# A three-phase decoder layer: self-attention body wrapped to sixteen steps, cross-attention steps reordered, combining stage split over three engines

## Chip, cores and metric

The kernel runs on one core of a Trainium2 chip. The metric is the device time of one execution in microseconds, lower is better. A core has a matrix engine (PE), and three engines for the rest: DVE (VectorE), ACT (ScalarE) and POOL (GpSimd). SP is the queue that issues transfers. Engines run their own instruction lists in order and wait for each other through semaphores.

## What is computed

Sixteen sequences of 256 tokens with 256 features pass through one decoder layer. Cut to its steps:

```python
def layer(x, ctx, mask):
    xn   = layer_norm(x) * w + b
    q, k, v, p, y = split(xn @ W_in.T + b_in)       # 16 heads of 32, k smeared with the token before
    pos  = cumsum(sigmoid(y))                       # forget gates, an additive bias of the scores
    a    = causal_softmax(q @ k.T * scale + pos) @ v * silu(p)
    x1   = layer_norm(x + layer_norm(a @ W_out.T))
    kv   = cat(layer_norm(ctx), layer_norm(x1))     # 512 keys, those of ctx under the mask
    o    = softmax(q2(x1) @ k2(kv).T / 8) @ v2(kv)  # 16 heads of 64
    x2   = layer_norm(x1 + o @ Wo)
    out  = layer_norm(x2 + moe(x2))                 # 8 experts, the best two of each token
```

## The kernel before

Three functions follow each other: `self_phase`, `cross_phase`, `expert_phase`. Each phase but the last loops over the 16 sequences, one pass for each. Products that need more than one float32r pass are split products: an operand is kept as a high and a low part, and three products replace one (L783 in the self-attention, L1566 in the cross-attention). Transposes, value products and the output projection are whole float32 products.

**Self-attention.** A pass has a step for each of 16 units (a unit is one head) and a few more steps in which nothing but the last units' tail is left. PE in a step: a piece of a projection of the next sequence (L783), transposes of probabilities (`transposes`, L831), the scores of the next unit (L823), and after each fourth unit a value product (L842, L849). ACT takes exponentials (L431) and transposed probabilities (L437), and takes the projections out of PSUM. DVE masks scores (L673, L675), gates, takes values and normalises. The next sequence's input is transposed (L791) near the start of a pass; its first user is the product L774, which reads `xn_t`.

**Cross-attention.** A pass has 32 units (one of 16 heads, one half of the queries) in 16 pairs, and 19 steps on PE; I write, with the lines of before, for pair i:

- S(i): the scores of pair i, six split products (`scores`, L1633). It fills both score banks, so it waits until the masked scores of pair i-1 are done.
- M(i): two masked copies on DVE, from the banks into two slots of `prob` (`masked_scores`, L1409), with the reciprocal of pair i-1's sums between them and two multiplications behind them (`probabilities`, L1420). ACT follows with the exponentials (L1219).
- T(i): eight transposes of pair i's probabilities (`transposes`, L1645), which ACT copies out (L1225). V(m): a value product after every second pair (`values`, L1662).
- P: a piece of a split projection of the next sequence (L1566), `kq`, `first` and `second` in the code.

PE runs T(i-2) and S(i+1) in step i. The `prob` slots form a ring of six, three pairs. So a masked copy also waits for transposes:

```python
apart(pt_filled, pt_filled.at(b, u - PROB_RING + 1))
apart(score_filled, score_filled.at(b, u + 1))
```

For pair i that is T(i-3), which PE runs in the same step as S(i). DVE carries other work between the pairs: the sum and statistics of the layer norm in step 3, `best_two` (the routing choice) in step 8, `list_places` in step 10. ACT takes the transposed context and latents in steps 4 and 5 (L1247, L1251).

**Experts.** After the expert rounds, a combining stage goes over 16 blocks: DVE adds the two expert rows and x2 (L2178, L2183), takes statistics (L2188, L2192) and normalises (L2200); POOL computes the reciprocal root.

Of the kernel before, what the change touches and what calls it, by code (L numbers as in the profile page):

```python
# [12 lines left out]
ALU = mybir.AluOpType  # L13
# [58 lines left out]
def decoder_layer(nc, x, ctx_in, mask, w_in_t, w_out_t, wq, wkv, wout, cols, rows, heads_rows, y_bias, wr,  # L72
                  w1, b1, w2, b2, out):
    x1_dram = nc.dram_tensor("x1_rows", (T + S, D), F32).ap()
# [3 lines left out]
    with stack:  # L78
# [14 lines left out]
        with ExitStack() as inner:  # L93
# [16 lines left out]
            cross_phase(nc, sem, passed, sig, ctx_in, mask, x1_dram, x2_dram, list_dram, ident, vx, pt, wq_s, wkv_s, wox, wr_s, col,  # L110
# [4 lines left out]
def self_phase(nc, sem, passed, sig, x, w_in_t, w_out_t, wq, wkv, wout, wr, cols, rows, heads_rows, y_bias, x1_dram, list_dram,  # L115
# [4 lines left out]
    XT, YP, QP, WO, KP, PP, VP = 0, 1, 2, 4, 6, 8, 10  # L120
    LNS = LN_X, LN_OUT, LN_RES = range(3)
    PROB_RING, PT_RING = 6, 2 * EC
    with ExitStack() as stack:
# [53 lines left out]
        v_a = sb("v_a", [P, TC, D_EXP])  # L177
        p_tanh = sb("p_tanh", [P, EC, S])
# [11 lines left out]
        x_res = sb("x_res", [P, TC, D])  # L190
        out_s = sb("out_s", [P, TC, D])
        centred = sb("centred", [P, TC, D])
# [16 lines left out]
        x_loaded, again_loaded = sig("x_loaded", 16), sig("again_loaded", 16, 0)  # L209
        parts_loaded = [sig(f"parts_loaded{g}", 16 * 8) for g in range(HPC)]  # L210
        x1_stored = sig("x1_stored", 16)
# [12 lines left out]
        zx_ready, x_res_ready, x1_ready = sig("zx_ready", 1), sig("x_res_ready", 1), sig("x1_ready", 1)  # L224
# [12 lines left out]
        gate_scaled = sig("gate_scaled", HPC)  # L237
        pt_filled = sig("pt_filled", HEADS)
# [9 lines left out]
        def gate_columns_of(w, k):  # L248

            return w[:, k, 3 * D_EXP:4 * D_EXP].rearrange("p (m g d) -> p g m d", g=HPC, m=EC)  # L250

# [4 lines left out]
        def _(sp):  # L256
# [14 lines left out]
            def spread_q_and_pos(b, g):  # L271
                sp.wait_ge(score_filled.sem, score_filled.at(b, EC * g + EC))
                spread_to(q_parts, g, (q_hi, q_lo, q_hi))
# [4 lines left out]
            def spread_early(b):  # L278

                sp.wait_ge(q_split.sem, q_split.at(b, 2))  # L280
                sp.wait_ge(pos_steps.sem, pos_steps.at(b, 4))
                for g in range(HPC - 1):
                    spread_q_and_pos(b, g)
                sp.wait_ge(k_split.sem, k_split.at(b, 2))
                for g in range(HPC - 1):
                    spread_to(k_parts, g, (k_hi, k_hi, k_lo))

            def spread_last(b):
                g = HPC - 1
                spread_q_and_pos(b, g)  # L290
                spread_to(k_parts, g, (k_hi, k_hi, k_lo))
# [13 lines left out]
            spread_early(-1)  # L305
            spread_last(-1)
# [5 lines left out]
            with sp.Fori(0, B) as b:  # L312
                pass_wait(zx_ready, zx_ready.at(b, 1))
                sp.dma_start(x_raw[:], rows_of((b + 2) % B)).then_inc(x_loaded.sem, 16)
                pass_wait(x_res_ready, x_res_ready.at(b, 1))
                sp.dma_start(x_again[:], rows_of(b)).then_inc(again_loaded.sem, 16)
                spread_early(b)
                pass_wait(x1_ready, x1_ready.at(b, 1))
                sp.dma_start(x1_dram.rearrange("(b c p) d -> b p c d", c=TC, p=P)[b], x1[:]).then_inc(x1_stored.sem, 16)
                spread_last(b)  # L320
            sp.wait_ge(x1_ready.sem, x1_ready.at(B, 1))
            sp.dma_start(x1_dram.rearrange("(b c p) d -> b p c d", c=TC, p=P)[B], x1[:]).then_inc(x1_stored.sem, 16)
# [3 lines left out]
            sp.wait_ge(x_loaded.sem, x_loaded.at(B, 16))  # L326
            for g in range(HPC):
                sp.wait_ge(parts_loaded[g].sem, parts_loaded[g].at(B - 1, parts_loaded[g].per))
# [3 lines left out]
        def _(pool):  # L332
# [41 lines left out]
            def residual(b):  # L374

                pool.wait_ge(again_loaded.sem, again_loaded.at(b, 16))
                pool.wait_ge(residual_ready.sem, residual_ready.at(b - 1, 1))
                pool.tensor_tensor(x_res[:], x_again[:], onb.unsqueeze(1).broadcast_to([P, TC, D]), ALU.add).then_inc(x_res_ready.sem, 1)

            pool.sem_inc(x_res_ready.sem, 1)  # L380
            for s in (var_ready, rstd_ready):
                for ln in (LN_OUT, LN_RES):
                    pool.sem_inc(s[ln].sem, 1)
            reciprocal_root(-1, LN_X)
            pool.wait_ge(in_weights, N_IN)
            low_q(-1)
            low_k(-1)
            reciprocal_root(0, LN_X)
            with pool.Fori(0, B) as b:
                residual(b)  # L390
                low_q(b)
                for ln in (LN_OUT, LN_RES):
                    reciprocal_root(b, ln)
                low_k(b)
                reciprocal_root(b + 1, LN_X)
            residual(B)
            for ln in (LN_OUT, LN_RES):
                reciprocal_root(B, ln)
# [3 lines left out]
        def _(act):  # L402
# [49 lines left out]
            def take_q(b, n):  # L452
                f = QP + n
                if n == 0:
                    act.wait_ge(q_split.sem, q_split.at(b - 1, 2))
                    for g in range(HPC):
                        act.wait_ge(parts_loaded[g].sem, parts_loaded[g].at(b - 1, parts_loaded[g].per))
                filled(b, f)
                for dst in (q_t, q_hi):
                    for i in range(2):  # L460
                        m = 2 * n + i
                        ins = nc.scalar.activation(dst[:, m, :], proj[f % 2][:, i * S:(i + 1) * S], ACT.Identity,
                                                   bias=q_bias[:, m:m + 1], scale=q_scale[:, m:m + 1])
                taken(ins, f)
# [10 lines left out]
            def high_k(b, n):  # L475
                f = KP + n
                act.wait_ge(proj_taken[f % 2].sem, proj_taken[f % 2].at(b, f // 2 + 1))
# [19 lines left out]
            def projections(b):  # L497
                take_xt(b)
                take_y(b)
                for n in range(2):  # L500
                    take_q(b, n)
                for n in range(2):
                    smear_k(b, n)
                    high_k(b, n)
                for n in range(2):
                    tanh_p(b, n)

            for s in (exp_ready, *pt_taken):
                act.sem_inc(s.sem, s.per)
            projections(-1)  # L510
            steps = {1: [take_xt], 2: [take_y], 3: [lambda b: take_q(b, 0)], 4: [lambda b: take_q(b, 1)],
                     5: [take_output(0)], 6: [take_output(1)], 7: [lambda b: smear_k(b, 0)], 9: [lambda b: smear_k(b, 1), lambda b: high_k(b, 0)],
                     11: [lambda b: high_k(b, 1)], 12: [lambda b: tanh_p(b, 0)],
                     14: [lambda b: tanh_p(b, 1)]}
            with act.Fori(0, B) as b:
                for i in range(HEADS + 3):
                    if i < HEADS:
                        exps(b, i)
# [1803 lines left out]
```

## Time and profile before

| | us |
|---|---|
| median of 3 runs (2789.85 to 2791.23) | 2791.01 |
| the profiled execution | 2794.18 |
| its span, first to last instruction | 2792.4 |
| PE busy, share of the span | 2442.5 (87%) |
| DVE busy | 1903.6 (68%) |
| ACT busy | 1736.8 (62%) |
| POOL busy | 806.5 (29%) |

The mean granted clock of TensorE was 0.956 of full speed. Time zero of the rows is the first instruction; an idle time in brackets stands ahead of the instruction and names what ended it. A matmul's own length overlaps with the next one, so the distance between two starts is what a piece of work costs PE.

### The profile page before, as it was taken

The page shows a single profiled execution, that of the slowest core. Times are in us where ns is not written, and L with a number is a line of the kernel's source. Part 1 is how long each engine was busy: PE and PEld are TensorE (multiplying, and loading weights), DVE is VectorE, ACT ScalarE, POOL GpSimd, SP SyncE. Part 2 cuts the span into 40 slices and gives each one's busy share as a digit, 9 for nine tenths or more (in the row PEclk, how much of TensorE's full clock was granted, in tenths as well). Part 3 has the DMA queues.
Part 4 walks back from the last instruction along what each step waited for, and adds up shares of the span by engine and source line. Part 5 has one row for each costly group of instructions (what it writes and reads, how often), then busy time and mean ns, then how long its engine had stood idle before and what let it go on. Part 6 is the DMA issues. An engine that isn't in the chain of part 4 may idle for free. (4 is left out here: it accounts for less than half of the span.)

```text
span 2792.4 us, 62033 instructions
## 1 busy us (share of the span) xinstructions
PE 2442.5 (87%) x18114; PEld 2021.8 (72%) x18114; DVE 1903.6 (68%) x5382; ACT 1736.8 (62%) x4354; POOL 806.5 (29%) x852
## 2 busy tenths in 40 slices
PE   5878887887599999999999999999999469999990
PEld 3666666666477777777777777777777369999990
DVE  4676667666556677666776667766677268888857
ACT  3777777777445666666666666666566156767650
POOL 1221212211333332333222332223332224444422
PEclk8999999999799999999999999999999789999995
DMA  5644544544300000000000000000000167777746
GB/s 143 151 98 106 113 94 113 113 95 111 80 16 9 9 15 16 16 15 2 16 16 16 16 4 14 15 16 16 9 9 15 43 197 237 233 233 236 234 148 229
DMA packets 162415, 228.14 MB, mean 82 GB/s; under 512 B 34544, under 2 KB 129136, under 8 KB 161776
## 3 DMA queue, kind: packets, MB, share of 16 engines
q1 hardware_dynamic: 151248, 205.85, 26.6%
q0 software_dynamic: 9664, 20.53, 2.1%
q14 instruction: 105, 0.86, 0.1%
q10 hardware_dynamic: 1376, 0.54, 0.1%
q8 instruction: 22, 0.36, 0.1%
HBM read 140.71 MB, written 23.74 MB: 59 GB/s over the span
## 5 line engine op out<-in xcount | busy, mean ns | idle before, releaser
L1409 DVE CUSTOM_DVE_ANT_0 x_prob<-x_score,x_mask_add 128x512 f32<-128x512 f32 x512 | 348.0, 682 | 275.4 <-PE x_score L1633 216.5
L1219 ACT ACTIVATE x_prob<-x_prob,x_low 128x512 f32<-128x512 f32 x512 | 366.9, 720 | 208.5 <-DVE x_low L1409 205.9
L1225 ACT COPY x_pt<-x_ptb 128x512 f32<-128x512 f32 x512 | 273.0, 584 | 240.9 <-PE x_ptb L1645 237.9
L1146 POOL TENSOR_TENSOR x_k_lo<-x_whole,x_k_hi 128x512 fp32r<-128x512 f32 x136 | 174.9, 1286 | 440.5 <-ACT x_k_hi L1265 438.1
L431 ACT ACTIVATE prob<-prob,low 128x128 f32<-128x128 f32 (+1 forms) x512 | 229.9, 455 | 103.8 <-DVE low L675 103.8
L1420 DVE TENSOR_SCALAR x_prob<-x_prob,x_rden 128x512 f32<-128x512 f32 x512 | 281.3, 591 | 0.6
L1645 PE MATMUL x_ptb<-ident,x_prob 128*128 128x128 f32 x2048 | 266.2, 273 | 0.0
L1662 PE MATMUL x_av<-x_pt,x_vx 128*64 128x256 f32 x2048 | 249.3, 385 | 0.0
L1645 PEld LDWEIGHTS x_ptb<-ident,x_prob 128*128 128x128 f32 x2048 | 230.3, 141 | 7.9 <-issue 5.8
L1389 DVE COPY x_whole<-x_proj 128x512 f32<-128x512 f32 x204 | 138.6, 686 | 128.5 <-PE x_proj L1566 127.0
L1662 PEld LDWEIGHTS x_av<-x_pt,x_vx 128*64 128x64 f32 x2048 | 135.7, 136 | 99.2 <-issue 43.8
L2026 ACT ACTIVATE h_t<-h_bank,b_s 128x256 f32<-128x256 f32 x312 | 130.8, 470 | 114.5 <-PE h_bank L2245 106.1
L2245 PE MATMUL h_bank<-xg_hi,w_hi 128*128 128x256 f32 x624 | 177.5, 284 | 21.5 <-DVE xg_lo L2106 20.1
L2245 PE MATMUL h_bank<-xg_hi,w_lo 128*128 128x256 f32 x624 | 177.3, 284 | 0.0
L2245 PE MATMUL h_bank<-xg_lo,w_hi 128*128 128x256 f32 x624 | 177.2, 284 | 0.0
L2259 PE MATMUL y_bank<-w_hi,h_hi 128*128 128x256 f32 x624 | 176.7, 283 | 0.0
L2259 PE MATMUL y_bank<-w_lo,h_hi 128*128 128x256 f32 x624 | 175.2, 281 | 0.0
L2259 PE MATMUL y_bank<-w_hi,h_lo 128*128 128x256 f32 x624 | 174.7, 280 | 0.0
L1566 PE MATMUL x_proj<-x_keys_hi,x_wkv_hi 128*128 128x256 f32 x544 | 164.4, 302 | 7.8 <-POOL x_keys_lo L1132 5.7
L1981 POOL DMA_INDIRECT expert_rows<-y_s,tokens x78 | 100.5, 1289 | 244.7 <-DVE y_s L2141 226.6
L673 DVE CUSTOM_DVE_ANT_0 prob<-score,causal 128x128 f32<-128x128 f32 x256 | 73.7, 288 | 124.8 <-PE score L823 119.3
L437 ACT COPY pt<-ptb 128x384 f32<-128x384 f32 x256 | 118.9, 471 | 64.0 <-PE ptb L831 64.0
(264 smaller groups left out, 7320.5 us busy)
## 6 DMA issues: line engine op xcount, KB each, us to landing
w_s<-w SPq DMA_DIRECT2D x156, 512.0 KB, 4.7
q_parts<-q_hi SPq DMA_DIRECT2D x136, 128.0 KB, 2.4
k_parts<-k_hi SPq DMA_DIRECT2D x136, 128.0 KB, 2.3
q_parts<-q_lo SPq DMA_DIRECT2D x68, 128.0 KB, 2.4
k_parts<-pos_parts SPq DMA_DIRECT2D x136, 64.0 KB, 2.4
k_parts<-k_lo SPq DMA_DIRECT2D x68, 128.0 KB, 2.4
w_s<-expert_rows SPq DMA_DIRECT2D x16, 512.0 KB, 4.3
b_s<-b SPq DMA_DIRECT2D x39, 128.0 KB
```

Source lines behind the costliest of these rows:

```text
L431: ins = nc.scalar.activation(s, s, ACT.Exp, bias=low[:, u, c:c + 1], scale=-1.0, accum_out=den[:, u, c:c + 1])
L1146: pool.tensor_tensor(part_of(n, q_lo, k_lo), whole_of(n), part_of(n, q_hi, k_hi).bitcast(F32), ALU.subtract).then_inc(low_ready.sem, 1)
L1219: nc.scalar.activation(slot, slot, ACT.Exp, bias=low[:, u:u + 1], scale=-1.0, accum_out=den[:, u:u + 1]).then_inc(exp_ready.sem, 1)
L1225: nc.scalar.copy(pt[:, u % PX_RING, :], ptb[u % 2][:, :]).then_inc(pt_taken[u % 2].sem, 1)
L1389: taken(dve.tensor_copy(whole[:, n % WHOLES, :], proj[f % 2][:, :]), f)
L1409: dve.tensor_tensor_reduce(prob[:, u % PROB_RING, :], score[u % 2][:, :], mask_add[:, :], -X_SCALE, 3.0e38, ALU.add, ALU.min, low[:, u:u + ...
L1420: ins = dve.tensor_scalar(slot, slot, rden[:, u:u + 1], None, ALU.mult)
L1566: ins = matmul(out, lhs(i, k), rhs(j, k), start=(k == 0 and i + j == 0), stop=(k == KC - 1 and i == 1))
L1645: ins = transpose(ptb[o][:, n * P:(n + 1) * P], prob[:, u % PROB_RING, n * P:(n + 1) * P], ident[:])
L1662: ins = matmul(av[m % 2][DH_X * o:DH_X * (o + 1), 0:S], vx[:, n, DH_X * h:DH_X * (h + 1)], pt[:, u:u + 3:2, n * P:(n + 1) * P], start=(n = ...
L2245: ins = matmul(h_bank[m][:, n * SLOTS:(n + 1) * SLOTS], w[a][:, k, f * P:(f + 1) * P], xs[z][:, k, :], start=(k == 0 and a + z == 0), stop ...
L2259: ins = matmul(y_bank[i][:, c * D:(c + 1) * D], h[a][:, f, c * P:(c + 1) * P], w[z][:, f, :], start=(f == 0 and a + z == 0), stop=(f == FC ...
```

## The change

**Self-attention.** The loop body has exactly 16 steps. With a lag of three, the transposes, the values and the takes of units 13 to 15 stand in the first steps of the next pass. The output chain (projection, statistics, residual, x1, store) of a sequence moves one pass later, spread over the pass. Values go to `v_next` first and POOL copies them to `v_a`. The normalisations of x and x1, the low part of xn and the residual's bias move from DVE to POOL. The `prob` ring shrinks from 6 to 4. The last pass is written out by itself, without a next sequence's projections.

**Cross-attention.** In each PE step the scores of the next pair and the split products come first, then the transposes, values and the other whole products. The tables of DVE, ACT and POOL stay. The last pass is written out by itself, without a next sequence's projections and normalisations.

**Combining stage.** The x2 blocks are loaded early, into expert weight buffers that are no longer used. The normalisation moves from DVE to ACT, and POOL computes a shift beside the reciprocal root.

```diff
--- before
+++ after
@@ self_phase @@
-    XT, YP, QP, WO, KP, PP, VP = 0, 1, 2, 4, 6, 8, 10
+    XT, YP, KP, QP, WO, PP, VP = 0, 1, 2, 4, 6, 8, 10
-    PROB_RING, PT_RING = 6, 2 * EC
+    PROB_RING, PT_RING = 4, 2 * EC
+    LAG = 3
@@ self_phase, POOL @@
+            def low_x(b):
+                pool.wait_ge(xn_hi_ready.sem, xn_hi_ready.at(b, 1))
+                pool.tensor_tensor(xn_lo[:], xn_t[:], xn_hi[:].bitcast(F32), ALU.subtract).then_inc(xn_split.sem, 1)
+            def values_in_place(b):
+                pool.wait_ge(av_done.sem, av_done.at(b - 1, HPC))
+                for f in (VP, VP + 1):
...
+                    pool.tensor_copy(v_a[:, f - VP, :], v_next[:, f - VP, :]).then_inc(v_ready.sem, 1)
+            def x1_of(b):
+                reciprocal_root(b, LN_RES)
+                pool.wait_ge(x1_stored.sem, x1_stored.at(b, 0))
+                normalise(LN_RES, x1, res1, x1_ready, b)
@@ cross_phase, PE @@
-            before_ = {1: second[1], 2: second[2], 4: last_values_and_context, 5: latents_transposed, 6: x2_transposed,
-                       8: kq[1], 9: kq[2], 10: kq[3], 11: kq[4], 12: kq[6], 13: kq[7], 14: kq[8], 15: kq[9], 16: kq[10],
-                       17: kq[11], 18: first[3]}
-            after_ = {0: second[0], 1: output, 6: kq[0], 7: logits, 9: prefixes, 11: kq[5], 13: first[0], 15: first[1],
-                      17: first[2]}
+            split_parts = {0: [second[0]], 1: [second[1]], 2: [second[2]], 4: [second[3]], 7: [kq[0]], 8: [kq[1]], 9: [kq[2]],
+                           10: [kq[3]], 11: [kq[4], kq[5]], 12: [kq[6]], 13: [kq[7], first[0]], 14: [kq[8]], 15: [kq[9], first[1]],
+                           16: [kq[10]], 17: [kq[11], first[2]], 18: [first[3]]}
+            whole_parts = {1: [output], 4: [context_transposed, latents_transposed], 5: [x2_transposed], 7: [logits], 9: [prefixes]}
             scores(0, 0)
-            with pe.Fori(0, B) as b:
+            def one_pass(b, split, whole, more):
                 for i in range(HEADS + 3):
-                    if i in before_:
-                        before_[i](b)
+                    if i + 1 < HEADS:
+                        scores(b, i + 1)
+                    elif i == HEADS + 2 and more:
+                        scores(b + 1, 0)
+                    for part in split.get(i, ()):
+                        part(b)
                     if 2 <= i < HEADS + 2:
                         transposes(b, i - 2)
-                    if i + 1 < HEADS:
-                        scores(b, i + 1)
-                    elif i == HEADS + 1:
-                        scores(b + 1, 0)
                     if i >= 4 and i % 2 == 0:
                         values(b, (i - 4) // 2)
-                    if i in after_:
-                        after_[i](b)
+                    for part in whole.get(i, ()):
+                        part(b)
...
+            with pe.Fori(0, B - 1) as b:
+                one_pass(b, split_parts, whole_parts, True)
+            one_pass(B - 1, {0: [second[0]], 1: [second[1]], 2: [second[2]], 4: [second[3]]},
...
@@ expert_phase, SP @@
+            for b in range(BLOCKS):
+                load_x2(b)
+            for n, tiles in enumerate((N_TILES - RING, N_TILES - RING, N_TILES - RING + 1)):
+                sp.wait_ge(h_filled.sem, h_filled.at(tiles, FC // 2))
+                for b in range(BLOCKS * (n + 1), BLOCKS * (n + 2)):
+                    load_x2(b)
```

The first place is PE's list in the cross-attention, step 10 of a pass (`x_score` rows are S(11), `x_ptb` rows T(8), `x_av` rows V(3), `x_proj` rows P). Before, the last product of the step's P stands first:

```order
L1566 MATMUL x_proj<-x_keys_hi,x_wkv_lo 128x256
L1643 REGISTER_ALU
L1645 MATMUL x_ptb<-ident,x_prob 128x128 x8
L1625 REGISTER_ALU
L1633 MATMUL x_score<-x_k_hi,x_q_hi 128x512 x2
L1633 MATMUL x_score<-x_k_hi,x_q_lo 128x512 x2
L1633 MATMUL x_score<-x_k_lo,x_q_hi 128x512 x2
L1662 MATMUL x_av<-x_pt,x_vx 64x256 x8
```

And now, from the end of the step's P to the scores of the next step, S(12); S(11) stands ahead of that P:

```order
L1680 MATMUL x_proj<-x_keys_hi,x_wkv_lo 128x256
L1757 REGISTER_ALU
L1759 MATMUL x_ptb<-ident,x_prob 128x128 x8
L1776 MATMUL x_av<-x_pt,x_vx 64x256 x8
L1739 REGISTER_ALU
L1742 REGISTER_ALU
L1747 MATMUL x_score<-x_k_hi,x_q_hi 128x512 x2
L1747 MATMUL x_score<-x_k_hi,x_q_lo 128x512 x2
L1747 MATMUL x_score<-x_k_lo,x_q_hi 128x512 x2
```

The scores have moved from behind the transposes to the head of the step, so between T(8) and the scores that need the pair after it there is now only V(3), and in odd steps nothing.

The second place is PE's list at the start of a self-attention pass (`ptb` rows are transposes of probabilities, `score` rows scores, `proj` rows the transposed input and the product that first reads it). Before:

```order
L788 REGISTER_ALU
L791 MATMUL proj<-ident,zx 128x128 x4
L819 REGISTER_ALU
L823 MATMUL score<-k_parts,q_parts 128x256 x2
L766 REGISTER_ALU
L774 MATMUL proj<-xn_t,win_y 16x256 x2
L819 REGISTER_ALU
L823 MATMUL score<-k_parts,q_parts 128x256 x2
```

And now:

```order
L896 MATMUL ptb<-ident,prob 128x128 x3
L884 ISA
L888 MATMUL score<-k_parts,q_parts 128x256 x2
L826 ISA
L853 REGISTER_ALU
L856 MATMUL proj<-ident,zx 128x128 x4
L893 REGISTER_ALU
L894 REGISTER_ALU
L896 MATMUL ptb<-ident,prob 128x128 x3
L884 REGISTER_ALU
L888 MATMUL score<-k_parts,q_parts 128x256 x2
```

The transposes of units 13, 14 and 15 of the sequence before now stand in the first three steps, and the product that reads `xn_t` comes two steps after the transposed input instead of one.

## Rows read from the trace of the kernel before

**Rows 1.** Windows: stretch, length, busy PE, PEld, DVE, ACT, POOL, clock, DMA share, GB/s:
```profile
56.74:728.28 671.54, 539.55 (x4146) 442.11 (x4150) 459.27 (x1852) 507.34 (x1664) 146.28 (x176) 0.96 0.49 114
728.28:745.10 16.82, 6.07 (x32) 4.45 (x24) 6.54 (x18) 0.74 (x2) 1.85 (x4) 0.73 0.13 28
...
969.37:2180.68 1211.31, 1194.05 (x8486) 922.24 (x8488) 836.80 (x2407) 765.95 (x1792) 354.12 (x365) 1.00 0.04 13
```

**Rows 2.** Groups of one cross-attention pass: the masked scores on DVE:
```profile
L1409 DVE CUSTOM_DVE_ANT_0 x_prob<-x_score,x_mask_add 128x512 f32<-128x512 f32 x33 | 22.4, 682 | 20.3 <-PE x_score L1633 13.4 <-issue 6.6
```

**Rows 3.** Timeline of PE, cross-attention, steps 10 and 11: start, length, instruction:
```profile
1363.56 1.04 PE L1645 MATMUL x_ptb<-ident,x_prob 128*128 128x128 f32 x8
1364.53 0.50 PE L1633 MATMUL x_score<-x_k_hi,x_q_hi 64*128 64x512 f32 x2
...
1365.43 1.95 PE L1662 MATMUL x_av<-x_pt,x_vx 128*64 128x256 f32 x16
1367.31 0.39 PE L1566 MATMUL x_proj<-x_keys_hi,x_wkv_hi 128*128 128x256 f32 x1
...
1368.83 0.60 PE L1645 MATMUL x_ptb<-ident,x_prob 128*128 128x128 f32 x4
```

**Rows 4.** Timeline of PE and ACT, step 8: transposes and their take:
```profile
1353.71 1.04 PE L1645 MATMUL x_ptb<-ident,x_prob 128*128 128x128 f32 x8
...
1354.35 1.07 ACT L1225 COPY x_pt<-x_ptb 128x512 f32<-128x512 f32 x2 [0.56 <-PE x_ptb L1645]
```

**Rows 5.** Timeline of DVE, cross-attention: pass start, steps 3, 8, 10:
```profile
1314.44 0.69 DVE L1409 CUSTOM_DVE_ANT_0 x_prob<-x_score,x_mask_add 128x512 f32<-128x512 f32 x1 [3.01 <-issue]
...
1333.20 0.67 DVE L1409 CUSTOM_DVE_ANT_0 x_prob<-x_score,x_mask_add 128x512 f32<-128x512 f32 x1
...
1336.71 0.69 DVE L1409 CUSTOM_DVE_ANT_0 x_prob<-x_score,x_mask_add 128x512 f32<-128x512 f32 x1
...
1353.91 0.69 DVE L1389 COPY x_whole<-x_proj 128x512 f32<-128x512 f32 x1 [0.21 <-PE x_proj L1566]
...
1358.46 0.69 DVE L1409 CUSTOM_DVE_ANT_0 x_prob<-x_score,x_mask_add 128x512 f32<-128x512 f32 x1
...
1364.38 0.68 DVE L1389 COPY x_whole<-x_proj 128x512 f32<-128x512 f32 x1
...
1367.22 0.68 DVE L1409 CUSTOM_DVE_ANT_0 x_prob<-x_score,x_mask_add 128x512 f32<-128x512 f32 x1
```

**Rows 6.** Timeline of PE: the score products of step 3:
```profile
1334.01 0.49 PE L1633 MATMUL x_score<-x_k_hi,x_q_hi 64*128 64x512 f32 x2 [0.67 <-DVE x_low L1409]
```

**Rows 7.** Timeline of ACT, cross-attention, steps 4 and 5:
```profile
1339.82 1.03 ACT L1247 ACTIVATE x_zctx<-x_proj,col 128x256 f32<-128x256 f32 x2
...
1341.40 0.72 ACT L1219 ACTIVATE x_prob<-x_prob,x_low 128x512 f32<-128x512 f32 x1
...
1342.82 1.05 ACT L1225 COPY x_pt<-x_ptb 128x512 f32<-128x512 f32 x2
```

**Rows 8.** Timeline of ACT, self-attention, from one pass to the next:
```profile
429.83 0.20 ACT L431 ACTIVATION_READ_ACCUMULATOR prob<-prob,low 128x1 f32 x1
431.31 0.48 ACT L437 COPY pt<-ptb 128x384 f32<-128x384 f32 x1 [1.28 <-PE ptb L831]
...
434.99 0.40 ACT L431 ACTIVATE prob<-prob,low 128x128 f32<-128x128 f32 x1 [0.60 <-DVE low L675]
```

**Rows 9.** Timeline of PE, self-attention: wait for the transposed input:
```profile
439.37 1.89 PE L774 MATMUL proj<-xn_t,win_y 128*16 128x256 f32 x4 [2.10 <-ACT xn_t L442]
```

**Rows 10.** Window of the self-attention right after that wait (columns as Rows 1):
```profile
439.30:441.00 1.70, 1.63 (x4) 0.43 (x4) 1.00 (x2) 1.52 (x6) 0.00 (x0) 0.50 0.32 113
```

**Rows 11.** Timeline of DVE, combining stage: one block and the next:
```profile
2734.68 0.71 DVE L2200 TENSOR_SCALAR ob<-res,mv,rstd 128x256 f32<-128x256 f32 x2
2735.31 0.87 DVE L2178 SCALAR_TENSOR_TENSOR half_sum<-w_s,gates,xb 128x256 f32<-128x256 f32 x2
...
2738.82 0.87 DVE L2178 SCALAR_TENSOR_TENSOR half_sum<-w_s,gates,xb 128x256 f32<-128x256 f32 x2
```

More of the change, by code:

```diff
@@ L401, in _ @@
+            with pool.Fori(0, B - 1) as b:
+                one_pass(b, True)
+            one_pass(B - 1, False)
+            for b in (B - 1, B):
+                reciprocal_root(b, LN_OUT)
+                residual(b)
+                x1_of(b)
         @block.scalar
@@ L542, in _ @@
             dve.memset(gated_t, 0.0)
+            for part in (prob, pt, v_a, out_s):
+                dve.memset(part[:], 0.0)
+            dve.memset(den[:], 1.0)
             dve.memset(one_keep[:], 1.0).then_inc(consts_v, 1)
@@ new lines, in _, with one_pass @@
+            last = {**steps, 4: steps[4][:1], 6: steps[6][1:], 7: [], 9: steps[9][:1], 10: [], 13: steps[13][:1], 14: steps[14][1:]}
+            def one_pass(b, parts):
+                for i in range(HEADS):
+                    masked_scores(b, i)
+                    for part in parts[i]:
+                        part(b)
+            with dve.Fori(0, B - 1) as b:
+                one_pass(b, steps)
+            one_pass(B - 1, last)
+            one_over_sums(B - 1, 3)
+            widen(B - 1, 3)
@@ L896, in _, with one_pass @@
+            scores(0, 0)
+            def one_pass(b, before, after):
+                for i in range(HEADS):
+                    if i in before:
+                        before[i](b)
+                    transposes(*unit(b, i - LAG))
                     if i + 1 < HEADS:
                         scores(b, i + 1)
-                    elif i == HEADS + 2:
+                    elif before:
                         scores(b + 1, 0)
-                    if i >= EC + 3 and (i - EC - 3) % EC == 0:
-                        values(b, (i - EC - 3) // EC)
@@ L904, in _ @@
+            for i in range(LAG + 1):
+                if i < LAG:
+                    transposes(*unit(B, i - LAG))
+                group_over(B, i)
             for f in range(WO):
@@ L1306, in _ @@
                         take_values(b, (i - 5) // 2)
-                    for part in steps.get(i, ()):
+                    for part in parts.get(i, ()):
                         part(b)
+            with act.Fori(0, B - 1) as b:
+                one_pass(b, steps)
+            one_pass(B - 1, last)
             take_x2_t(B)
@@ L1499, in _, with one_pass @@
                      17: [part(11)]}
-            with dve.Fori(0, B) as b:
+            last = {0: [last_values], 1: [v_part(V1, 1, 1)], 3: [residual_sum], 4: [v_part(V1, 3, 1), x2_of], 8: [best_two], 10: [list_places]}
+            def one_pass(b, parts):
                 for i in range(HEADS + 4):
@@ L1509, in _ @@
                         probabilities(b, i - 1)
-                    for part in steps.get(i, ()):
+                    for part in parts.get(i, ()):
                         part(b)
-            for part in (last_values, residual_sum, x2_of, best_two, list_places):
+            with dve.Fori(0, B - 1) as b:
+                one_pass(b, steps)
+            one_pass(B - 1, last)
+            for part in (residual_sum, x2_of, best_two, list_places):
                 part(B)
```

464 lines of the change are left out of this document (253 added, 211 removed).

## Prediction

> **What bounds the kernel now.** I first read the windows [rows 1]: the reader is to see that the self-attention passes fill 671.5 us (16 passes, 42.0 us each) with PE, DVE and ACT all between 68% and 80% busy, so that no engine bounds them, and that 14 cross-attention passes take 1211.3 us, 86.52 us each, with PE busy 98.6% of it at full clock. In the cross-attention PE is the bound, and what counts is whether it keeps being fed. Then I read the groups of one pass: the masked scores on DVE wait for the score products and never for transposes [rows 2]. Last the timelines, for what a step costs from start to start [rows 3]: a T takes .97 us, an S .90, a V 1.88, a P 1.52. PE waits for scores by .67 us in step 3 [rows 6]; all its idle time in a pass is 86.52 less 1194.05/14, 1.2 us [rows 1].
>
> **The change, cross-attention.** M(i) needs two things: the scores S(i), and the `prob` slots that T(i-3) empties. Both stand in the same PE step. Before, T(i-3) stood ahead of S(i), so its end was never waited for. Now S(i) comes first, then P, then T(i-3), then a V in even steps, and the next product on PE is S(i+1), which waits for M(i). So PE finishes T, and DVE can only then mask the pair that PE needs next. The chain from the start of T: its first half is seen by a waiting engine, ACT here, .64 us later [rows 4]; the second masked copy starts .69 us after the first (a copy's length) and S follows the start of the second copy by .81 us (1333.20 to 1334.01) [rows 5, 6]. That is 2.14 us from T's start, against .97 us that PE is busy with T: 1.17 us of waiting wherever T directly precedes S. A V behind T covers it (2.85 us).
>
> Step by step, the waits of one new pass:
> - S(4), S(13), S(15): T directly ahead, 1.2 each, 3.6. S(9) and S(11) have logits or prefixes (about .9 and 1.1 us) behind T: .3 and .1.
> - S(5): in step 3 DVE goes from one masked copy to the next pair in 3.51 us, for the layer norm [rows 5]. With .69 for the second copy, S(4) to S(5) is 4.20; PE has S and T, 1.87. Wait 2.3.
> - S(10): `best_two`. The P of step 8 now ends .90 + 1.52 = 2.42 after S(9) starts; its copy follows .20 later (1353.71 to 1353.91) [rows 4, 5], the next masked pair 4.55 after that (1358.46), and S 1.50 later: 8.67. PE has S, P, T and V, 5.27. Wait 3.4.
> - S(12): `list_places`, the same with 2.84 in place of 4.55 [rows 5]: 6.96 against 5.27. Wait 1.7.
> - S(7) and S(8): ACT takes context and latents ahead of the exponentials, 1.58 us each, and the exponentials take 1.42 a pair [rows 7]; DVE's reciprocal between the two masked copies needs them. The context's transposes end half a microsecond before S(6); from there 1.58, 1.42 and .81 make 3.8, which is 3.3 after S(6), and 3.6 with three hand-overs of about .1 (estimate). PE has S, T and four transposes, 2.4: wait 1.2. For S(8) the same sum, one pair on, leaves .5.
> - S(2): DVE starts a pass 3.01 us late, waiting for nothing the trace shows [rows 5]. S(2) now stands 1.5 us earlier in the list. Wait about .6.
>
> Sum 13.7 us. I add .8 because a late pair makes the next one late too, which step-by-step sums leave out: 14.5. Less the old 1.2, plus .5, PE loses **13.8 us a pass**. Fifteen passes: +207. The .5 is for two more switches between tile shapes in a pass (41 before, 43 now, counted in PE's list); its bounds are nothing and .5, since the rows don't isolate a switch and the first product of an S, .50 long, bounds one half of it [rows 3]. The Trainium skill, TensorEngine Tiling (Array Packing), section Key Properties, says that a change of tiling mode drains the engine; by it the new order, which groups by kind, would gain only if it had fewer switches, and it has not.
>
> The last pass drops 12 P of keys and queries and 4 of values (16 x 1.5 = 24 us) and two transposes (1 us), but most of its waits stay, about 13 us: 86.5 - .9 (waits and switches above) - 25 + 14 = 75 us, **-12**.
>
> **Self-attention.** From the last exponential of a pass to the first of the next ACT spends 429.83 to 434.99, 5.16 us, of it four takes at about .48 [rows 8]; the takes stay and 3.2 us go. PE waits 2.10 us for `xn_t` [rows 9]; with scores and transposes put ahead of its reader that wait goes, and with it the half clock of the stretch after it (.50, [rows 10]). Gain 5.3 us a pass less .1: 36.8. ACT's own busy time is 507.3/16 = 31.7 [rows 1], so 32 is the floor; if DVE's and POOL's moved work collides, 39. POOL is busy 146.3/16 = 9.1 us a pass [rows 1] and would have to grow threefold to bind: hidden by its idle time. SP's store of x1 and one set of transfers wait for later work, but their reader comes a pass later: hidden while POOL ends before the pass does; if not, about 1 us a pass. Fifteen passes: **-78**. The last one sheds the projections: 11 us of ACT's work, to 27 us: **-15**. Against it the units 13 to 15, a value product and two serial output chains stand behind the loop, where 16.8 us stood before [rows 1]: about 23, **+6**, and a longer start, **+1**. Sum **-86**.
>
> **Combining stage.** A block takes 3.51 us (2735.31 to 2738.82), of it .71 normalising, which leaves DVE [rows 11]. At best .6 a block for 16 blocks, less 1 us for the longer chain through POOL and ACT at the end: **-8.5**; nothing if transfers bound it. The early loads of x2 lie beside expert rounds and cost nothing.
>
> **Sum.** +207 - 12 - 86 - 8.5 = +100.5 on 2794.2, the profiled execution's own time, gives 2894.7; that execution is 3.2 above the median, so **2892 us**.
>
> **Rivals.**
> - *The waits are absorbed* (faster). If DVE and ACT run ahead enough that no pair is ever late, PE stays at 86.5 + .5 a pass, +7.5 in all, the last pass falls to 62, -24.5: 2791 + 7.5 - 24.5 - 86 - 8.5 = 2680. For it: DVE is busy 69% in a pass. Against it: the wait is one of order, not of load, since M(i) can't begin before T(i-3) whatever DVE did before. The change is faster in sum only if a pass loses less than (86 + 8.5 + 12)/15 = 7.1 us. Chance .06.
> - *Only the plain ring waits show* (also faster): 1.17 us in steps without a V, DVE's and ACT's long steps hidden. 5 us a pass, +75: 2791 + 75 - 12 - 86 - 8.5 = 2760. Against it: DVE's long pieces stand in its list between the pairs, and before they were met just in time, .67 us late [rows 6]. Chance .09, with all between 2760 and 2850.
> - *The forecast*, 2850 to 2950: .75.
> - *More than the forecast*, 2950 and up. PE's long waits lower its clock: in the self-attention a wait of 2.10 us is followed by a stretch at .50 of full clock, that is 1.2 GHz in place of 2.4 [rows 9, 10]. Two such waits a pass cost up to 3 us, +45. Or ACT's list, which now begins its cross-attention loop further on, pays at each pass what DVE pays, 3 us, of which perhaps 2 reach PE: +30. The Trainium skill, Runtime: NRT & Kernel Launch, section Instruction fetch mechanics, says that a branch out of the two pages loaded stalls for a fetch; DVE's 3.01 us agrees with it. Either gives 2920 to 2970. Chance .10.
>
> **How the numbers follow.** The forecast's own bounds come from the per-pass loss, 11 to 17.5 us (2850 to 2950), with the self-attention's 34 to 39 inside it. 2850 to 2955 holds about 8 in 10. A change of .2% or less, 5.6 us, is about what a measurement here can't tell from none. Faster by more: .06 and about half of the second rival, .11; within: .01; slower: .88.
>
> **What the profile after would show.** Right: cross-attention passes of about 100 us, PE busy near 86% there; the masked scores on DVE waiting for `x_ptb`, which never happened before; S waiting for DVE in nearly every odd step by 1.2 us, and by over 3 us at S(10); self-attention passes of 36 to 38 us; a combining block near 3 us. Wrong: passes of 87 us with the same waits as before would fell the central step; passes of 92 would say that DVE's long steps stay hidden; self-attention passes over 39 us would say that the wrapped body found a new wait, most likely POOL.

## The result and the profile after

The changed kernel takes **2983.41 us** (median of 4 runs, 2974.76 to 2988.04) against 2791.04 before: a ratio of 1.0687, with a 95% interval of 1.0662 to 1.0711. The direction was forecast, the size was not: 2892 was predicted, with a range to 2955. The changed kernel lost 192 us where 101 were forecast. The result, e1_old_order, e7_three_self and e9_values_early are medians of 4 or 5 executions; every other run below is a single one.

First the windows of the changed kernel, cut where PE's loops end a pass: 14 self-attention passes; then the last self-attention pass, the tail, the start of the cross-attention and its first pass; 14 cross-attention passes; the last one with the start of the experts; and, four expert rounds later, the rest.

```profile
core 0: us, PE busy (x) PEld busy (x) DVE busy (x) ACT busy (x) POOL busy (x), PEclk, DMA share, GB/s
...
94.24:674.83 580.59, 462.00 (x3644) 387.23 (x3644) 365.94 (x1555) 447.02 (x1457) 247.08 (x252) 0.96 0.47 108
674.83:876.65 201.82, 146.85 (x1005) 116.79 (x1002) 109.56 (x335) 95.81 (x240) 69.18 (x80) 0.87 0.11 31
876.65:2306.94 1430.29, 1237.86 (x8486) 950.32 (x8488) 809.88 (x2411) 763.36 (x1792) 364.06 (x365) 0.97 0.04 11
2306.94:2537.94 231.00, 160.63 (x1134) 137.65 (x1135) 126.25 (x278) 109.78 (x224) 50.14 (x53) 0.84 0.34 110
...
2820.47:2981.20 160.73, 101.19 (x863) 100.98 (x861) 112.03 (x218) 76.11 (x146) 62.97 (x94) 0.82 0.66 213
```

The reader is to see two divisions. 580.59/14 is 41.47 us for a self-attention pass, where 36.8 was forecast and 42.0 stood before [rows 1]. 1430.29/14 is 102.16 us for a cross-attention pass, where 100.3 was forecast and 86.52 stood before. The same cuts in the trace before give the ledger:

| stretch | before | after | change | forecast |
|---|---|---|---|---|
| start to the end of the first self-attention pass | 97.75 | 94.24 | -3.5 | -4 |
| 14 self-attention passes | 588.44 | 580.59 | -7.9 | -73 |
| last self-attention pass to the end of the first cross-attention pass | 196.65 | 201.82 | +5.2 | +5 |
| 14 cross-attention passes | 1211.33 | 1430.29 | +219.0 | +193 |
| last cross-attention pass to the end of the first expert round | 242.98 | 231.00 | -12.0 | -12 |
| four expert rounds | 281.44 | 282.53 | +1.1 | 0 |
| the rest, with the combining stage | 173.8 | 160.7 | -13.1 | -8.5 |
| span | 2792.4 | 2981.2 | +188.8 | +100.5 |

Of the 88 us that the forecast missed, 65 are in the 14 self-attention passes and 26 in the 14 of the cross-attention; the rest gives 3 back.

**Self-attention.** The timeline of PE in one pass of 41.20 us, only the rows with a wait ahead of them:

```profile
390.24 1.03 PE L839 MATMUL proj<-xn_t,win_y 128*16 128x256 f32 x4 [1.67 <-ACT xn_t L495]
392.29 0.36 PE L848 MATMUL proj<-xn_hi,win_hi 128*128 128x256 f32 x1 [1.02 <-POOL xn_lo L397]
...
400.20 0.39 PE L848 MATMUL proj<-xn_hi,win_hi 128*128 128x256 f32 x1 [1.98 <-DVE k_t L684]
...
403.64 0.58 PE L848 MATMUL proj<-xn_hi,win_hi 128*128 128x256 f32 x1 [0.40 <-DVE k_t L684]
...
409.69 2.00 PE L839 MATMUL proj<-wo,x_pt 128*128 128x256 f32 x8 [0.97 <-ACT q_hi L512]
...
414.11 1.97 PE L839 MATMUL proj<-wo,x_pt 128*128 128x256 f32 x8 [1.85 <-ACT q_hi L512]
...
422.81 0.50 PE L848 MATMUL proj<-win_hi,xn_hi 128*128 128x512 f32 x1 [0.51 <-ACT p_tanh L540]
```

The waits sum to 8.40 us, and PE is busy for the other 32.8. The same cut in the trace before shows that this isn't less waiting than there was:

```profile
97.75:686.19 588.44, 472.40 (x3644) 387.04 (x3640) 402.62 (x1626) 443.81 (x1456) 128.00 (x154) 0.96 0.47 106
```

There PE was idle for 116.0 us of 14 passes, 8.3 a pass; now it is 118.6, 8.5 a pass. PE's busy time fell by .7 us a pass and its idle time rose by .2. The wait for `xn_t` has gone from 2.10 [rows 9] to 1.67 and is not gone; POOL's low part of xn adds one of 1.02. The others are waits of a projection (L848) or an output (L839) for one of the two PSUM banks that all projections share: the bank is free only when DVE has taken the keys from it (1.98, .40), ACT the queries (.97, 1.85) or the gate's tanh (.51).

**Cross-attention.** The timeline of PE in a pass, its first long waits for masked scores: S(4), S(5) and S(7).

```profile
1305.64 0.50 PE L1747 MATMUL x_score<-x_k_hi,x_q_hi 64*128 64x512 f32 x2 [1.44 <-DVE x_low L1516]
...
1309.77 0.50 PE L1747 MATMUL x_score<-x_k_hi,x_q_hi 64*128 64x512 f32 x2 [2.14 <-DVE x_low L1516]
...
1319.95 0.50 PE L1747 MATMUL x_score<-x_k_hi,x_q_hi 64*128 64x512 f32 x2 [1.48 <-DVE x_low L1516]
```

And later in the same pass S(10), S(12) and S(13):

```profile
1337.69 0.80 PE L1747 MATMUL x_score<-x_k_hi,x_q_hi 64*128 64x512 f32 x2 [3.25 <-DVE x_low L1516]
...
1351.04 0.50 PE L1747 MATMUL x_score<-x_k_hi,x_q_hi 64*128 64x512 f32 x2 [0.82 <-POOL x_q_lo L1240]
...
1357.32 0.50 PE L1747 MATMUL x_score<-x_k_hi,x_q_hi 64*128 64x512 f32 x2 [1.36 <-DVE x_low L1516]
```

Set beside the sum of the prediction: 1.44 (1.2 forecast), 2.14 (2.3), 1.48 (1.2), 3.25 (3.4), .82 (1.7) and 1.36 (1.2). S(2) waits .73, S(8) .43, S(9) .57, S(15) 1.36. The row of S(12) names POOL, whose instruction ended at 1351.01; but the masked copy that S(12) needs starts at 1350.23, and S(12) follows it by .81, the distance of the prediction. So this too is read as a wait for DVE. The ten waits make 13.58 us; the step-by-step sum said 13.7.

The groups of that pass show whom DVE waits for:

```profile
L1516 DVE CUSTOM_DVE_ANT_0 x_prob<-x_score,x_mask_add 128x512 f32<-128x512 f32 x33 | 22.5, 683 | 17.1 <-PE x_ptb L1759 10.5 <-PE x_score L1747 5.1 <-issue 1.0
```

Before, DVE waited there for scores and never for transposes [rows 2]. Now 10.5 us of DVE's idle time ahead of the masked scores end with the transposes of `x_ptb`.

What the sum had not priced stands in four windows of 3 us around S(10) of the next pass (columns as above):

```profile
1436.65:1439.65 3.00, 0.07 (x2) 0.00 (x0) 2.75 (x10) 0.37 (x1) 0.85 (x1) 0.89 0.01 3
1439.65:1442.65 3.00, 2.68 (x11) 1.94 (x12) 1.06 (x4) 1.15 (x4) 0.00 (x0) 0.50 0.00 0
1442.65:1445.65 3.00, 3.00 (x16) 3.00 (x16) 0.69 (x1) 0.28 (x1) 0.00 (x0) 0.50 0.00 0
1445.65:1448.65 3.00, 2.89 (x23) 2.40 (x22) 2.23 (x7) 2.84 (x8) 0.77 (x1) 0.97 0.00 0
```

PE is idle for nearly the whole first window, and the granted clock is at half, 1.2 GHz, in the two behind it. This happens behind 13 of the 14 waits of S(10). Two further passes show that the wait alone doesn't decide it: behind a wait of 2.14 us ahead of S(5) the clock falls in 3 of the 14 passes (first row below), and behind the 3.26 us of one S(10) it stays at full speed (second and third row):

```profile
1104.65:1107.65 3.00, 2.90 (x9) 1.97 (x10) 0.84 (x4) 0.92 (x4) 0.00 (x0) 0.50 0.00 0
...
1642.00:1645.00 3.00, 0.00 (x0) 0.00 (x0) 2.75 (x12) 0.62 (x1) 0.60 (x1) 1.00 0.01 3
1645.00:1648.00 3.00, 2.93 (x23) 2.52 (x24) 1.11 (x5) 0.90 (x4) 0.00 (x0) 1.00 0.00 0
```

**Combining stage.** The timeline of DVE, one block and the next:

```profile
2933.58 0.85 DVE L2325 SCALAR_TENSOR_TENSOR half_sum<-w_s,gates,xb 128x256 f32<-128x256 f32 x2
...
2936.33 0.85 DVE L2325 SCALAR_TENSOR_TENSOR half_sum<-w_s,gates,xb 128x256 f32<-128x256 f32 x2
```

One block follows another by 2.75 us, the first by 2.78. Before, two blocks were 3.51 apart [rows 11], but later ones up to 4.1: the mean distance was 3.65. So .9 us a block is saved, not .6.

### The profile page after: what moved, and what is told of

Its sections match the earlier page's. It is cut to its first block and busy times, and to the rows that moved or that the text cites. A ratio compares the mean times of both kernels' runs of the same rounds, so it can differ in the third digit from the quotient of the medians.

```text
span 2981.2 us, 61036 instructions
## 1 busy us (share of the span) xinstructions
PE 2444.2 (82%) x17865; PEld 2018.9 (68%) x17865; DVE 1803.4 (60%) x5239; ACT 1734.9 (58%) x4347; POOL 950.8 (32%) x983
## 5 line engine op out<-in xcount | busy, mean ns | idle before, releaser
L1747 PE MATMUL x_score<-x_k_hi,x_q_hi 64*128 64x512 f32 x512 | 132.4, 513 | 216.6 <-DVE x_low L1516 201.6
L1759 PE MATMUL x_ptb<-ident,x_prob 128*128 128x128 f32 x2048 | 278.6, 281 | 0.2 <-ACT x_pt L1325 0.2
L1759 PEld LDWEIGHTS x_ptb<-ident,x_prob 128*128 128x128 f32 x2048 | 240.5, 145 | 32.1 <-DVE x_prob L1527 10.9
L1747 PEld LDWEIGHTS x_score<-x_k_hi,x_q_hi 64*128 64x128 f32 x512 | 49.4, 189 | 290.5 <-DVE x_low L1516 209.5
L1527 DVE TENSOR_SCALAR x_prob<-x_prob,x_rden 128x512 f32<-128x512 f32 x512 | 243.0, 517 | 0.6
```

The lines of the kernel that those rows point to most:

```text
L1527: ins = dve.tensor_scalar(slot, slot, rden[:, u:u + 1], None, ALU.mult)
L1747: ins = matmul(score[o][:, :], (q_hi, q_lo)[a][rows, m, tokens], (k_hi, k_lo)[z][rows, m, :], start=(a + z == 0), stop=(z == 1))
L1759: ins = transpose(ptb[o][:, n * P:(n + 1) * P], prob[:, u % PROB_RING, n * P:(n + 1) * P], ident[:])
```

## Experiments

### The order of the cross-attention undone

Label e1_old_order. The changed kernel, in each PE step the scores back behind the transposes, and the tables of before:

```diff
-                    if i + 1 < HEADS:
-                        scores(b, i + 1)
-                    elif i == HEADS + 2 and more:
-                        scores(b + 1, 0)
                     for part in split.get(i, ()):
                         part(b)
                     if 2 <= i < HEADS + 2:
                         transposes(b, i - 2)
+                    if i + 1 < HEADS:
+                        scores(b, i + 1)
+                    elif i == HEADS + 1 and more:
+                        scores(b + 1, 0)
```

> The changed kernel with the cross-attention's PE steps put back in the order of before (transposes, then scores); everything else of the change stays. Theory (the order alone costs the cross-attention 15.8 us a pass, 13.6 of them waits for masked scores and about 3 a lower clock): passes of 86.5 us again in place of 102.3, the last one about 12 us shorter than in the changed kernel, so 2983 - 15 x 15.8 - 12 = 2735 us, some 2% faster than before. Rival (part of the loss comes from other parts of the change, such as the place of the loops in the program): passes stay above 90 us and the time above 2790.

Measured: 2741.82 us, ratio to before .9825 (.9807 to .9843). The windows over 14 passes each, self-attention and cross-attention:

```profile
94.11:672.05 577.94, 459.24 (x3644) 384.89 (x3644) 366.17 (x1555) 446.61 (x1457) 247.23 (x252) 0.96 0.48 108
857.00:2067.61 1210.61, 1193.36 (x8486) 922.16 (x8488) 813.16 (x2411) 764.55 (x1792) 357.85 (x365) 1.00 0.04 13
```

1210.61/14 is 86.47 us a pass, at full clock. So the rest of the change gains about 50 us, and with the new order the whole loses 192.

### The order alone

Label e10_order_alone. The kernel before with only the new tables and the new order.

> The kernel before with nothing changed but the order of the cross-attention's PE steps. Theory (the order costs 15.8 us a pass by itself, in 16 passes): 2791 + 16 x 15.8 = 3044 us, passes of 102.3. Rival (part of it comes only together with the other changes): under 3000.

Measured: 3043.66 us, passes of 102.4 in the mean of 15, against 102.2 in the changed kernel. The order makes this loss by itself.

### Eight slots in the ring

Label e2_ring8, and the same kernel again as e8_cross_only.

```diff
-    PROB_RING = 6
+    PROB_RING = 8
```

> The changed kernel with eight slots in the cross-attention's ring of probabilities in place of six; the order of the steps stays changed. Theory (in odd steps the masked copies wait for the slots that T(i-3) empties): those waits of 1.4 us go, DVE waits for transposes no more, the waits behind DVE's and ACT's long steps (S(5), S(10), S(12)) stay, PE's waits fall from 13.6 to about 8.5 us a pass, the pass from 102.3 to about 97, the time to about 2905. Rival (the masked copies are late because of DVE's own work and the exponentials alone): no change.

> The ring of eight slots a second time, to see whether its cross-attention passes of 98.9 us and its lower clock in two places of a pass come again. Theory (a wait of 1.9 us or more after a thin stretch lets the clock fall, whichever product it stands ahead of): passes again 98.5 to 99.2 us. Rival (the clock of a single execution is chance): passes differ by over 1 us from the first run.

Measured: 2917.15 and 2918.31 us, passes of 98.87 both times. The groups of a pass in the first of the two:

```profile
L1516 DVE CUSTOM_DVE_ANT_0 x_prob<-x_score,x_mask_add 128x512 f32<-128x512 f32 x33 | 22.4, 682 | 13.3 <-PE x_score L1747 11.8 <-issue 1.2
```

DVE no longer waits for transposes at all. PE doesn't wait ahead of S(4), S(13) and S(15) any more, and S(5), S(7) and S(10) still wait 1.87, 1.47 and 3.28, behind DVE's and ACT's long steps. This is the ring's part of the waits, 4.6 us, and it is shown by taking away the ring's limit alone. The pass shortened by 3.3 us and not by the 5.3 expected. The window of the next pass says why:

```profile
1357.91:1456.87 98.96, 89.98 (x608) 69.40 (x610) 57.92 (x173) 54.26 (x128) 25.24 (x27) 0.95 0.04 11
```

PE is busy 90.0 us, at a mean clock of .95, where the changed kernel has 88.6 at .97. The clock falls twice in a pass here, behind the wait of S(10) in all 14 passes and behind the 1.87 us of S(5) in 13. The repeat has the same busy time and clock: this is not chance in this kernel. That such a wait always does it, as the expectation of the repeat supposed, is not so; e11_ring_and_best has the same wait ahead of S(5) with one fall in 14 passes.

### The routing ahead of the take

Label e3_best_first.

```diff
-                     ... 8: [part(1), best_two], 9: [part(2)],
+                     ... 8: [best_two, part(1)], 9: [part(2)],
```

> The changed kernel with best_two ahead of the take of a projection in DVE's step 8. Theory (PE's longest wait, 3.25 us ahead of S(10), comes from best_two waiting behind that take, and the clock falls only after this wait): the wait shrinks to 1.4 us, the clock of the stretch behind it stays at full speed, PE busy falls from 88.6 to about 85.5 a pass, the pass from 102.3 to about 97.3, the time to about 2908. Rival (the clock falls because PE is idle 13% of the pass, whichever wait it is): PE busy stays near 88, the pass is about 100.4, the time 2955.

Measured: 2917.79 us, passes of 98.4 in the mean. The wait ahead of S(10) is .39 us, 1 us less than the 1.4 expected: one comparison in `best_two` (`x_is_best`, its second use) takes 1.17 us in the changed kernel and .17 here. Why isn't shown. Two windows of neighbouring passes, a usual one and one of the two short ones:

```profile
1359.79:1458.39 98.60, 87.58 (x608) 66.71 (x610) 56.96 (x173) 54.42 (x128) 26.09 (x27) 0.98 0.04 11
```

```profile
1262.71:1359.79 97.08, 86.00 (x608) 65.78 (x610) 57.03 (x174) 54.40 (x128) 26.09 (x27) 1.00 0.04 12
```

The second has the same work and the same waits within .1 us, and a clock of 1.00 throughout: 97.08 us. The first is 1.5 us longer and has a stretch at half clock, right behind the wait of S(5), 2.14 us in both passes:

```profile
1383.79:1386.79 3.00, 3.00 (x10) 1.93 (x7) 0.18 (x1) 0.27 (x2) 0.00 (x0) 0.50 0.00 0
```

So with that wait the fall behind S(10) is gone, but one behind the shorter wait of S(5) takes its place in 12 of the 14 passes, where the changed kernel had it in 3. The rival was half right: it isn't one wait alone.

### Both cross-attention edits

Label e11_ring_and_best.

> The changed kernel with eight slots in the ring and best_two ahead of the take, the two cross-attention edits together. Theory (the ring's waits and best_two's wait are separate: 3.3 us and 3.7 us a pass): passes of about 95 us, time about 2860. Rival (without both waits something else of DVE is late): passes of 97 or more.

Measured: 2829.03 us. The window over 14 passes:

```profile
870.70:2160.80 1290.10, 1202.35 (x8486) 921.70 (x8488) 802.62 (x2411) 757.64 (x1792) 352.84 (x365) 1.00 0.04 12
```

1290.10/14 is 92.15 us, where the two single gains added up would give 95.1. The waits do add up, in the mean of 14 passes: 4.8 us of idle PE go with the ring and 2.7 with `best_two`, and 7.5 with both (13.7 to 6.3). The rest is PE's busy time: 88.4 us in the changed kernel, 89.9 with the ring alone, 87.4 with `best_two` alone, and 85.9 here, at a clock of 1.00. Against 85.3 busy before [rows 1], this also bounds the two extra switches between tile shapes: at most .6 us a pass. Of the 15.6 us that a pass lost, 5.6 are left, 5.0 of them waits, the longest ahead of S(5) (1.86) and S(7) (1.48).

### Outputs later, input earlier, keys earlier

Three single edits to the self-attention of the changed kernel, then all three on top of the old cross-attention order. Labels e4_outputs_late (with ACT's takes of the outputs one step later too), e5_input_early, e6_keys_early:

```diff
-... 9: outputs[0], 10: outputs[1], 11: p_chunks[0],
+... 10: outputs[0], 11: lambda b: (outputs[1](b), p_chunks[0](b)),
```

```diff
-            steps = {1: [take_xt], 3: [take_y],
+            steps = {0: [take_xt], 3: [take_y],
```

```diff
-                     5: [lambda b: widen(b, 0), lambda b: gate(b - 1, 3)],
-                     6: [lambda b: take_k(b, 0), lambda b: centred(b - 1)],
-                     7: [lambda b: take_k(b, 1)],
+                     5: [lambda b: take_k(b, 0), lambda b: widen(b, 0), lambda b: gate(b - 1, 3)],
+                     6: [lambda b: take_k(b, 1), lambda b: centred(b - 1)],
+                     7: [],
```

> The changed kernel with the two output projections of the self-attention one step later on PE (10 and 11 in place of 9 and 10) and their takes one step later on ACT. Theory (a self-attention pass stays at 41.2 us because PE waits for its two projection banks, here 0.97 and 1.85 us for the takes of the queries): these two waits go and the pass falls by 1.5 to 2.8 us, the time by 25 to 40. Rival (the body is bound elsewhere, and the wait only moves): passes within 0.5 us of 41.2.

> The changed kernel with ACT's take of the transposed input one step earlier (step 0 in place of 1). Theory (a self-attention pass is as long as PE's work, 32.8 us, plus its waits, 8.4 us; two of these, 1.67 for xn_t and 1.02 for its low part, follow from ACT taking the input behind the exponentials of step 1): the take starts about 1.4 us earlier, both waits shrink to under 1.3 together, the pass falls from 41.2 to about 39.8. Rival (the waits are slack that the next one takes over): within 0.5 us of 41.2.

> The changed kernel with DVE's two takes of the keys at the head of step 5 and in step 6 (before: 6 and 7), ahead of the widening and the gate. Theory (PE's wait of 1.98 us in step 6 is for the projection bank that DVE empties there): that wait falls below 0.7 us and the pass from 41.2 to about 39.9. Rival (the gate and the value product come later and hold PE instead): within 0.5 us of 41.2.

Measured, as the mean of 14 passes: 40.63, 40.15 and 39.37 us against 41.3 to 41.5; the times were 2979.25, 2972.24 and 2959.82 us. The first gave .8 us, less than the 1.5 expected: the waits for the queries' banks went, and other waits of .99, .70 and .61 stood in their place. The second removed the wait for the low part of xn, but the wait of 1.67 stayed, now for another bank:

```profile
420.28 1.03 PE L839 MATMUL proj<-xn_t,win_y 128*16 128x256 f32 x4 [1.67 <-DVE v_next L712]
...
429.18 0.38 PE L848 MATMUL proj<-xn_hi,win_hi 128*128 128x256 f32 x1 [1.98 <-DVE k_t L684]
```

The third cut the wait for the keys' bank from 1.98 to .19 and lengthened the first one for the queries' from .97 to 1.76:

```profile
421.96 0.38 PE L848 MATMUL proj<-xn_hi,win_hi 128*128 128x256 f32 x1 [0.19 <-DVE k_t L684]
...
430.64 1.99 PE L839 MATMUL proj<-wo,x_pt 128*128 128x256 f32 x8 [1.76 <-ACT q_hi L512]
```

Label e7_three_self, all three with the old cross-attention order:

> The changed kernel with the old order of the cross-attention and all three self-attention edits (outputs later, input taken earlier, keys taken earlier). Theory (the waits for banks and the input are separate and add up): self-attention passes of about 38 us in place of 41.3, the time 2742 - 15 x 3.3 = 2692 us. Rival (they share one slack): passes of 40 us or more, 2720 us or more.

Measured: 2680.48 us, ratio .9596 (.9575 to .9617). The waits of a pass over .2 us, the first three of them, and the window over 14 passes:

```profile
394.75 1.03 PE L839 MATMUL proj<-xn_t,win_y 128*16 128x256 f32 x4 [1.67 <-DVE v_next L712]
...
401.89 0.38 PE L848 MATMUL proj<-xn_hi,win_hi 128*128 128x256 f32 x1 [0.22 <-DVE k_t L684]
...
409.66 0.55 PE L896 MATMUL ptb<-ident,prob 128*128 128x128 f32 x3 [0.82 <-ACT pt L490]
```

```profile
95.16:608.66 513.50, 445.31 (x3644) 370.43 (x3643) 360.30 (x1555) 443.43 (x1457) 239.12 (x252) 1.00 0.53 120
```

513.50/14 is 36.68 us a pass, better than the 38 expected. The single gains below 41.5 add up to 4.3 us, the three together give 4.6 below the 41.3 of e1_old_order. That is the sum or a little more; single executions and two starting points that differ by .2 don't decide which. The granted clock is 1.00 where it was .96.

### Values earlier

Label e9_values_early: `take_v(b - 1, 1)` at the head of DVE's step 1 in place of step 2, on top of the last one.

> The kernel with the old cross-attention order and the three self-attention edits, and DVE's take of the second half of the values at the head of step 1 in place of step 2. Theory (the last long wait of a self-attention pass, 1.67 us ahead of the product that reads xn_t, is now for the projection bank that this take empties): the wait shrinks below 0.5 us, the pass falls from 36.7 to about 35.4, the time from 2680 to about 2661. Rival (the gate behind it comes later, and the value product of step 3 or the exponentials hold PE): within 5 us of 2680.

Measured: 2672.36 us, ratio .9580 (.9567 to .9594), passes of 36.1. The wait of 1.67 is gone, and the wait for POOL's low part of xn, which it had covered, is back at the same place:

```profile
391.30 0.36 PE L848 MATMUL proj<-xn_hi,win_hi 128*128 128x256 f32 x1 [1.05 <-POOL xn_lo L397]
```

This is the fastest version found, 118 us below the kernel before. Half of the expected gain went to the wait next in line.

## Why the prediction was wrong in size

- **"Gain 5.3 us a pass less .1: 36.8" is the step that failed**, for 65 of the 88 us. It added a gap on ACT (3.2 us) and a wait of PE (2.10), as if both lay on one chain, took them off the old pass and kept the rest as it was. But PE was idle for 8.3 us of the old pass, of which that wait is a quarter, and the new order of chunks, takes and outputs made its own: 8.5 us in the mean, in the pass shown seven waits of 8.4, five of them (5.7 us) for a PSUM bank. Even the wait for `xn_t`, which was to go, stayed at 1.67; e5_input_early shows a bank behind it, which the values hold. I had not asked of each projection who frees its bank and in which step. The measured pass was 41.5. That the body can run at 36.7, once takes and outputs stand in other steps, is what e7_three_self shows. That this is nearly the predicted 36.8 is chance: its pass still holds 4.5 us of waits, the 1.67 ahead of the reader of `xn_t` among them, and the half clock is gone. The half clock, which was to go too, is still in the changed kernel's mean of .96. I named "passes over 39" as the sign of a new wait, but guessed POOL; it was mainly the banks, and POOL had 1.0 us of it.
- **PE loses 13.8 us a pass in the cross-attention.** The mechanism stood: e1_old_order and e10_order_alone give it both ways, e2_ring8 shows the ring's part, e3_best_first the part of `best_two`. The waits were priced at 13.7 and measured at 13.58. S(12) was overpriced (1.7 against .82) and S(4), S(7), S(9) and S(13) underpriced by .2 to .3 each. The miss at S(12) is one cast in `list_places`, first before, then now:

```profile
1366.02 1.26 DVE L1471 CAST x_slot_i<-x_slot_f 128x4 int32<-128x4 f32 x1
...
1349.16 0.17 DVE L1578 CAST x_slot_i<-x_slot_f 128x4 int32<-128x4 f32 x1
```

Its median over the run is 1.26 us before and .17 in the changed kernel, so the 2.84 us of the prediction became 2.03. What makes it long isn't shown. The .8 for lateness handed on did not appear; nothing in the ten waits asks for it. It made up by luck for a part of what was left out, the clock.
- **The clock** was put among the rivals, at up to 3 us a pass and a chance of .10. It costs 2.7 in the pass shown: PE is busy 88.6 us there and 85.9 in e11_ring_and_best at full clock. So the loss is 13.6 - 1.2 + .6 + 2.7 = 15.7 us against the 13.8 predicted, and in the mean of 14 passes 15.6. A mechanism that the trace before shows in its own rows, half clock behind a wait of 2.1 us, belonged into the sum as soon as the sum held waits of 2.3 and 3.4. The .5 for switches agrees with the .6 at most that the runs leave for them. The Trainium skill, TensorEngine Tiling (Array Packing), section Key Properties, says that a change of tiling mode drains the engine. These runs bound what two of them cost and isolate none.
- **None of the rivals held the largest miss.** The one that allowed more than the forecast had the clock and ACT's loop start, and its times end at 2970, below the measured 2983.
- **ACT's loop start**, the other part of that rival, did not come: at the start of a cross-attention pass ACT is idle for 1.93 us, and what ends that is PE's value product. DVE's late start stays: 2.81 to 3.09 us of idle time ahead of the first masked copy of a pass, 2.82 to 3.13 before, though the trace now names the score product as what ended it. The Trainium skill, Runtime: NRT & Kernel Launch, section Instruction fetch mechanics, says that a taken branch whose target lies outside the two loaded pages stalls for a fetch. The 3 us of DVE agree with that, ACT shows no such start, and no run isolates it.
- **The last passes and the tail**: forecast +5 and -12, measured +5.2 and -12.0. The +5 is a sum of -15, +6 and 13.8 whose parts weren't measured apart. If the first cross-attention pass lost 15.6 us like the others, the other parts came out some 2 us better than forecast, so the close match is in part chance.
- **The combining stage** was undersized: -8.5 against -13.1. I took .6 a block off the distance of two early blocks, and the measured .9 is off a longer mean. From start to start, the normalisation that left DVE is .63 of it; the rest is about .1 each between the two additions and between the statistics and their aggregate, ahead of which DVE waited .15 before. No row shows DVE waiting for x2 in these blocks, before or after, so the early loads have no part that the trace shows; no run takes them out alone.

What stays open: what lets the clock fall behind a wait in one pass and not in the next. S(5) waits 2.14 us in all 14 passes of the changed kernel and the clock falls behind it in 3; the same wait in e3_best_first has 12 falls in 14. In e2_ring8 it is 1.87 us with 13 falls in 14, in e11_ring_and_best 1.86 with 1 in 14. And one of the changed kernel's 14 waits ahead of S(10) has none.

## What to carry to other kernels

When a step is reordered, look for waits that close through a ring: the slot that an engine needs may be freed by the very block that is now behind it, and no free time elsewhere covers that; more slots did, for 4.6 of the 13.6 us here. When a loop is wrapped or shortened, list for each block who frees its output bank and in which step; a pass is as short as that table allows, not as short as its busiest engine. And if the sum contains PE waits as long as one that already lowers the clock in the trace, price a slow stretch behind them.

## What the runs showed of the hardware

The granted clock fell to 1.2 GHz behind 13 of 14 waits of 3.25 us in the changed kernel, and behind shorter ones in some passes only: 3 of 14 and 12 of 14 waits of 2.14 us in two kernels, 13 of 14 and 1 of 14 waits of 1.87 and 1.86 us in two others. So in these runs the length of the wait by itself doesn't tell whether the clock falls. A fall made a pass 1.5 us longer in e3_best_first; in the changed kernel it cost 2.7. Three edits that cut the waits of a self-attention pass from 8.4 to 4.5 us brought its mean clock from .96 to 1.00, and PE's busy time from 33.0 to 31.8.

Two small DVE instructions of the cross-attention took 1 us more in some kernels than in others, at the same shape: the cast of `list_places` 1.26 us in median before and .17 in the changed kernel, the second `x_is_best` 1.17 in the changed kernel and .17 in e3_best_first. The cause is open.
